# Conditioned transformer block and rotation: the first batch's projections and maxima are moved in the program order

## The reference, cut to what matters

```python
ada = silu(c) @ W_ada + b_ada
shift_msa, scale_msa, gate_msa, shift_mlp, scale_mlp, gate_mlp = split(ada, 6)
h = layernorm(x) * (1 + scale_msa) + shift_msa
x = x + gate_msa * attention(h)          # softmax(q k^T / 3) v, 16 heads, then W_proj
h = layernorm(x) * (1 + scale_mlp) + shift_mlp
x = x + gate_mlp * (gelu(h @ W_fc1 + b_fc1) @ W_fc2 + b_fc2)
U, _ = qr(P)                             # P: 144 x 64
R = expm(A(silu(cond) @ W.T + b))        # A: skew-symmetric 64 x 64 for each batch
x_rot = x + (x U R - x U) U^T
```

## Time and profile before

| what | value |
|---|---|
| median of 3 runs | 350.19 us (350.04 to 352.31) |
| the profiled execution: its time | 352.32 us |
| the profiled execution: its span, first to last instruction | 350.5 us |
| PE busy | 288.3 us (82%), 2717 matmuls |
| DVE busy | 244.1 us (70%), 762 instructions |
| ACT busy | 145.0 us (41%) |
| POOL busy | 120.3 us (34%) |
| mean granted TensorE clock | 0.974 |

### The profile page before, as it was taken

The page is one execution under the profiler, slowest core; times in us unless marked ns, Lnnn a source line. Parts: engine busy times, 40 slices in busy tenths (PEclk is TensorE's granted clock), DMA queues, the critical chain, the costliest instruction groups (busy, mean ns, idle before and its releaser), DMA issues.

```text
span 350.5 us, 7754 instructions
## 1 busy us (share of the span) xinstructions
PE 288.3 (82%) x2717; PEld 175.1 (50%) x2717; DVE 244.1 (70%) x762; ACT 145.0 (41%) x270; POOL 120.3 (34%) x307
## 2 busy tenths in 40 slices
PE   2897877598987877879888879888987999999774
PEld 1333443254434443545455545555756666666662
DVE  6758656866767888976888978986565555665541
ACT  2212102377776474544455554555431332122211
POOL 6730820700602639333525316233043433310010
PEclk9999999999899999987999999999999999999995
DMA  4924230231551232220221210000000000000013
GB/s 124 287 61 137 57 91 9 51 79 37 131 160 29 60 88 46 56 74 17 67 75 34 72 52 3 4 2 3 2 2 1 1 2 0 3 0 2 0 35 102
DMA packets 20285, 18.00 MB, mean 51 GB/s; under 512 B 3541, under 2 KB 18087, under 8 KB 20122
## 3 DMA queue, kind: packets, MB, share of 16 engines
q1 hardware_dynamic: 19314, 16.31, 17.2%
q10 hardware_dynamic: 934, 1.21, 1.2%
HBM read 12.32 MB, written 4.81 MB: 49 GB/s over the span
## 4 chain that ended last, share of the span: by engine, by line
PE 48%; DVE 40%; issue 6%; ACT 3%; POOL 1%; DMA 0%; DVEq 0%; ACTq 0%; POOLq 0%
DVE nm L958 15%; PE ps L463 6%; PE m L497 6%; DVE gp L765 5%; PE pst L277 4%; PE m L299 4%; PE m L672 4%; PE m L283 3%; DVE gm L766 3%; PE pst L394 3%; PE pst L484 3%; DVE qst L801 2%; DVE piv L800 2%; PE pst L278 2%; DVE pm L795 2%
## 5 line engine op out<-in xcount | busy, mean ns | idle before, releaser
L958 DVE TENSOR_REDUCE nm<-ps 128x2 f32<-128x512 f32 x128 | 87.6, 688 | 33.2 <-PE ps L463 29.2
L1196 ACT ACTIVATE pex<-pst 128x1024 f32<-128x1024 f32 x64 | 65.6, 1025 | 28.2 <-PE pst L484 24.3
L463 PE MATMUL ps<-ks,qs 54*128 54x256 bf16 x256 | 28.1, 297 | 27.0 <-DVE nm L958 26.3
L497 PE MATMUL m<-pex,ve 128*32 128x256 f32 x512 | 36.0, 401 | 0.0
L795 DVE TENSOR_SCALAR pm<-m 64x1 f32<-64x1 f32 x64 | 13.6, 212 | 29.0 <-PE m L299 28.4
L1518 POOL TENSOR_TENSOR xin<-xin,res 128x288 f32<-128x288 f32 x16 | 12.7, 793 | 59.0 <-DVE res L987 59.0
L463 PEld LDWEIGHTS ps<-ks,qs 54*128 54x128 bf16 x256 | 10.3, 98 | 41.5 <-issue 36.8
L283 PE MATMUL m<-gm,ident 64*64 64x65 f32 x126 | 24.0, 278 | 7.0 <-DVE gm L766 3.9
L484 PE MATMUL pst<-qs,ks 56*128 56x256 bf16 x256 | 26.3, 284 | 1.4 <-ACT pex L1196 1.2
L283 PEld LDWEIGHTS m<-gm,ident 64*64 64x64 f32 x126 | 14.1, 157 | 26.3 <-issue 19.1
L1496 POOL TENSOR_TENSOR qkr<-qk,parts 96x768 f32<-96x768 f32 x6 | 9.8, 1637 | 46.5 <-ACT parts L1177 34.0
(11 more groups left out here) (253 smaller groups left out, 572.7 us busy)
## 6 DMA issues: line engine op xcount, KB each, us to landing
scr_qk<-parts SPq DMA_DIRECT2D x24, 144.0 KB, 2.0
qs<-scr_qk SPq DMA_DIRECT2D x96, 36.0 KB
ks<-scr_qk SPq DMA_DIRECT2D x72, 36.0 KB
gates<-scr_ada SPq DMA_DIRECT2D x2, 576.0 KB, 6.1
out_dram<-xin SPq DMA_DIRECT2D x8, 144.0 KB, 2.0
wr<-in_L_cond_W_dram SPq DMA_DIRECT2D x1, 1134.0 KB
xin<-in_x_dram SPq DMA_DIRECT2D x1, 864.0 KB, 5.4
ks<-scr_qk ACTq DMA_DIRECT2D x24, 36.0 KB
```

What stands on the lines that cost most here:

```text
L463: ins = mm(ps[e][:, L * i:L * i + L], qs[64 * e:64 * e + KS, b % 3, 2 * g + i, 128 * lt:128 * lt + 128], ks[64 * e:64 * e + KS, b % 3, 2 * ...
L497: last = mm(m[32 * j:32 * j + 32, 0:L], ve[:, t % 3, mt, 4 * g + j, :], pex[:, n % 4, 2 * e + i, :], start=(mt == 0), stop=(mt == LT - 1))
L958: nc.vector.tensor_reduce(nm[:, lt, e, 2 * g:2 * g + 2], ps[e][:, :].rearrange("p (h l) -> p h l", h=2), AX.X, ALU.max, negate=True).then_ ...
L1196: nc.scalar.activation(pex[:, n % 4, :, :], pst[0][:, :, :], ACT.Exp, scale=ATT_SCALE).then_inc(s("exp_done"), 1)
```

## The change

The number of chain steps in the prologue falls from 14 to 9. All 8 slots of turn -1 get one (before: the last 4), and the MLP half starts with 4 instead of 3, so that step 85 comes at its first turn as before; in turns 0 to 7 each slot holds the step that the slot before it held. On PE and DVE the first batch's three q and k chunks follow one another with no chain step between them, and so do the remainders and the split; the second batch's projections come after, one chunk for each of steps 3, 4 and 5. Its remainders and its split move from ahead of turn -1 into that turn's slots 0, 1 and 2. `values(0)` is cut in halves over slots 0 and 1; `values(1)` moves to turn 0, slot 2; the second `wrT` moves from slot 1 to slot 0 of turn 0. `modulation_rests` and ACT's copy of `msr` move into slot 2 of turn -1. GpSimd's memsets of `ve` move from the start to behind `normalise(1)`.

```diff
@@ -44,3 +44,3 @@
 
-    PROLOGUE_STEPS = 14
+    PROLOGUE_STEPS = 9
     N_BASIS = 6
@@ -48,3 +48,3 @@
     TAIL_STEPS = 7
-    FIRST_STEPS = 3
+    FIRST_STEPS = 4
 
@@ -231,4 +231,4 @@
 
-            at = PROLOGUE_STEPS + (t + 1) * NS + n - NS // 2
-            return range(at, at + 1) if (t, n) >= (-1, NS // 2) and at < CHAIN else range(0)
+            at = PROLOGUE_STEPS + (t + 1) * NS + n
+            return range(at, at + 1)
 
@@ -236,6 +236,6 @@
 
-            at = PROLOGUE_STEPS + NS // 2 + B * NS + (FIRST_STEPS + TAIL_STEPS * t if t >= 0 else 0) + i
+            at = PROLOGUE_STEPS + (B + 1) * NS + (FIRST_STEPS + TAIL_STEPS * t if t >= 0 else 0) + i
             return range(at, at + 1) if at < CHAIN else range(0)
 
-        BASIS_TURN = (R + 1 - PROLOGUE_STEPS - NS // 2) // NS
+        BASIS_TURN = (R - PROLOGUE_STEPS) // NS - 1
         EXPM = 3
@@ -247,3 +247,3 @@
 
-        TURNED = [(0, 7), (1, 6), (2, 5), (3, 5), (4, 5), (6, 5), (7, 5), (7, 6)]
+        TURNED = [(0, 7), (0, 5), (2, 5), (3, 5), (4, 5), (6, 5), (7, 5), (7, 6)]
 
@@ -431,2 +431,4 @@
                         pe.wait_ge(s("hTf_ready"), b + 1)
+                    elif b == 2:
+                        pe.wait_ge(s("wqk_stacked"), 4)
                 m = shared[bank]
@@ -441,5 +443,5 @@
 
-            def values(b, bank):
-                m = claim(pe, bank, "values", b)
-                for lt in range(LT):
+            def values(b, bank, halves=range(LT)):
+                m = claim(pe, bank, "values", b) if 0 in halves else shared[bank]
+                for lt in halves:
                     rows = slice(128 * lt, 128 * lt + 128)
@@ -449,3 +451,4 @@
                     last = project(m[:, C * lt:C * lt + C], hTa[:, b % 2, rows], hTr[:, b % 2, rows], wqkv_a[:, 2 * C:3 * C], wqkv_r[:, 2 * C:3 * C])
-                filled(last, "values", b)
+                if LT - 1 in halves:
+                    filled(last, "values", b)
 
@@ -534,8 +537,10 @@
                     if t == -1:
-                        if n == 0:
-                            values(0, 6)
-                        if n == 1:
-                            values(1, 7)
+                        if n < LT:
+                            values(0, 6, (n,))
+                        if n == 2:
+                            modulation_rests()
                         if n == 4:
                             shift(0, 0, 5)
+                    if t == 0 and n == 2:
+                        values(1, 6)
                     if n == 0 and real(t - 1):
@@ -605,17 +610,11 @@
                     transpose_h(0, 6)
-                if k == 3:
                     pe.wait_ge(s("wqk_ready"), 8)
                     qk("qk2", (2,), 0, 7)
-                if k == 4:
-                    qk("qk01", (0,), 0, 5, 0)
-                if k == 6:
-                    qk("qk01", (1,), 0, 5, 1)
+                    qk("qk01", (0, 1), 0, 5)
                     transpose_h(1, 6)
-                if k == 7:
-                    modulation_rests()
-                if k == 8:
+                if k == 3:
                     qk("qk2", (2,), 1, 7)
-                if k == 10:
+                if k == 4:
                     qk("qk01", (0,), 1, 5, 0)
-                if k == 12:
+                if k == 5:
                     qk("qk01", (1,), 1, 5, 1)
@@ -623,3 +622,2 @@
             pe.wait_ge(s("identb_ready"), 1)
-            pe.wait_ge(s("wqk_stacked"), 4)
             pe.wait_ge(s("hTf_ready"), 2)
@@ -711,2 +709,3 @@
             transpose_h(B + 2, 5)
+            chain(mlp_steps(-1, 3))
             for t in range(B):
@@ -1010,2 +1009,9 @@
                         by_token(t - 1, 1)
+                    if t == -1:
+                        if n == 0:
+                            rest_of("qk2", 1, 2, 1)
+                        if n == 1:
+                            rest_of("qk01", 1, 0, 2)
+                        if n == 2:
+                            split(1)
                     if n == 3:
@@ -1046,9 +1052,5 @@
                     statistics(range(2, 4), "mv_ready")
-                if k == 3:
-                    batch_rows()
-                if k == 4:
-                    rest_of("qk2", 0, 2, 1)
                     dve.wait_ge(s("pT_filled"), 1)
                     nc.vector.tensor_copy(pT[:, :], ps[0][0:R, 0:C]).then_inc(s("pT_ready"), 1)
-                if k == 6:
+                    rest_of("qk2", 0, 2, 1)
                     rest_of("qk01", 0, 0, 2)
@@ -1056,10 +1058,8 @@
                     last_channels(1)
-                if 7 <= k < 11:
-                    if k == 7:
+                if k == 3:
+                    batch_rows()
+                if 4 <= k < 8:
+                    if k == 4:
                         dve.wait_ge(s("x1_loaded"), 16)
-                    statistics(range(4 + 3 * (k - 7), 7 + 3 * (k - 7)), "mv_ready")
-                if k == 10:
-                    rest_of("qk2", 1, 2, 1)
-            rest_of("qk01", 1, 0, 2)
-            split(1)
+                    statistics(range(4 + 3 * (k - 4), 7 + 3 * (k - 4)), "mv_ready")
             for t in range(-1, B):
@@ -1221,7 +1222,7 @@
                     if t == -1:
-                        if n == 0:
-                            evac_values(0)
                         if n == 1:
-                            evac_values(1)
+                            evac_values(0)
                         if n == 2:
+                            act.wait_ge(s("msr_filled"), 1)
+                            nc.scalar.copy(msr[:, :, :, :].rearrange("p b i c -> p (b i c)"), st_bank[0][:, :]).then_inc(s("msr_ready"), 1)
                             stack_of_k(1)
@@ -1229,2 +1230,4 @@
                             shift(0, 0)
+                    if t == 0 and n == 2:
+                        evac_values(1)
                     if n == 0 and real(t - 1):
@@ -1263,9 +1266,7 @@
             evac_hT(1)
-            act.wait_ge(s("msr_filled"), 1)
-            nc.scalar.copy(msr[:, :, :, :].rearrange("p b i c -> p (b i c)"), st_bank[0][:, :]).then_inc(s("msr_ready"), 1)
             stack_of_k(0)
             high_part("qk2", 1, 2, 1)
+            high_part("qk01", 1, 0, 2)
             act.wait_ge(s("wstack_loaded"), 7 * 16)
             by_dimension(wqk_r, wqkv_r, "wqk_stacked")
-            high_part("qk01", 1, 0, 2)
             for t in range(-1, B):
@@ -1541,5 +1542,2 @@
             nc.gpsimd.memset(hTf, 1.0).then_inc(s("hTf_one"), 1)
-            nc.gpsimd.memset(ve[:, :, :, :, :], 0.0).then_inc(s("ve_zeroed"), 1)
-            pool.wait_ge(s("ve_zeroed"), 1)
-            nc.gpsimd.memset(ve[:, :, :, :, D:D + 1], 1.0).then_inc(s("ve_zeroed"), 1)
             nc.gpsimd.memset(onesb[:, :], 1.0).then_inc(s("ones_ready"), 1)
@@ -1560,2 +1558,5 @@
             normalise(1)
+            nc.gpsimd.memset(ve[:, :, :, :, :], 0.0).then_inc(s("ve_zeroed"), 1)
+            pool.wait_ge(s("ve_zeroed"), 1)
+            nc.gpsimd.memset(ve[:, :, :, :, D:D + 1], 1.0).then_inc(s("ve_zeroed"), 1)
             pool.wait_ge(s("mv_ready"), 6)
```

6 lines of the change are left out of this document (3 added, 3 removed).

## The result

| | median of | executions | us |
|---|---|---|---|
| before, as shown above | 3 | 350.04 to 352.31 | 350.19 |
| before, beside the changed kernel | 4 | 350.04 to 352.31 | 351.16 |
| changed | 4 | 354.87 to 357.60 | 356.51 |

What follows compares the result with a forecast made beforehand. No engine is full, so time was taken as a sum of hand-overs between engines. The terms -1.85, -1.2, +0.95, +0.75 and +1.4 sum to +0.05, put on the median of 350.19: 350.2, range 346.3 to 353.5.

Steps and rivals of the forecast that it cites:

- Start, -1.85: Kernel start: without the `ve` memset DVE's first operation ends earlier, first projection from 15.06 to 13.2; bounds 0 to 2.05.
- Prologue and turn -1: -1.2 more: DVE's first maximum at 35.5, much of that gain lost in turn -1; bounds -3.1 to +0.6.
- both waits: Turn -1: PE starts slot 4's maxima 0.6 late behind GpSimd; ACT's `evac_hT(2)` waits for GpSimd's constants, charged 0.55.
- Turn 0, +0.95: Turn 0: `values(1)` in slot 2 costs +2.0, moving one `wrT` to slot 0 gives -1.05.
- The wait of 2.10: DVE's idle time ahead of turn 0 slot 2's maximum; moving a `wrT` into slot 0 was to take 1.05 off.
- my slower rival (0.12): Turn 0: the clock rises two slots later, each slot of 2.6 grows by 2; 354.2, chance 0.12.
- Basis, +0.75: Turns 5 and 6: basis norms one slot later make PE wait 1.4 in turn 6's slot 1, half hidden; bounds 0 to 1.4.
- MLP entry, +1.4: Ahead of the MLP's turns: the added chain step repeats a round over DVE with PE idle; bounds 0.9 to 1.6.
- Elsewhere the order is the same, so I let later work move as one block.: Stretches whose order is unchanged, say turns 1 to 4, keep their length; a change by over 1 would be wrong.
- The sum: Whole kernel: -1.85 - 1.2 + 0.95 + 0.75 + 1.4 = +0.05 on a span of 350.5.
- I put the difference on the median: Whole time: the +0.05 is added to the median of 350.19, not the profiled 352.32, giving 350.2.

Runs made afterwards that it cites:

- the fillers: Eight unused bf16 matmuls per slot in turn -1's PE waits: on the changed kernel 351.47 and 349.49; with values(1), steps and norms also moved, 346.87 and 344.69.

## Why the prediction was wrong

- **Start, -1.85.** Right as a mechanism, and in size for the memset alone (-1.70). In the first profile only -0.8 came, since `hb` met GpSimd's subtraction; over four profiles the first projection is 1.55 earlier on average. What I left out is that `hb` moved into other GpSimd work, and that DVE's first operation has more than one outcome even with the memset in place.
- **Prologue and turn -1.** DVE's first maximum at 35.5 was forecast; the four profiles give 35.8 on average. From the first projection to it the forecast had 22.3, and all four profiles have 22.3. Slot 4, both waits, and turn 0's start (3.05 earlier forecast, 3.0 measured) were right in the first profile. In two others slot 7 took 2.68 and not 5.09, since DVE came ahead of GpSimd, and turn 0 began almost 7 earlier.
- **Turn 0, +0.95. This step failed.** The wait of 2.10 fell to 1.26, -0.84 of the -1.05. But `values(1)`, taken at 2.0 between bounds of 1.1 and 3.1, made the slot 4.7 to 4.8 longer in three of four profiles and 1.6 in one. The bounds held only the work moved in. With the clock still low behind it, the rest of the slot was paid at 1.2 GHz too: L500 1.94 for 1.07, L351 1.10 for 0.65, the maxima 0.64 for 0.39, together 1.6. It is close to my slower rival (0.12), which put it down to a PE gap in slots 1 and 2. No gap was needed: PE was busy without a break from 65.1 to 76.3, the rise, all at the low clock.
- **Basis, +0.75.** PE waits for GpSimd 1.4, as forecast, in every profile. With the clock up, the stretch is nonetheless 0.4 shorter than before (14.56 for 14.94); with the low clock that followed the wait in three of four it is 1.1 longer. The mean of +0.8 fits the forecast by accident.
- **MLP entry, +1.4.** The round costs 1.4, as forecast. Missing were the 1.5 of low clock behind PE's gap, there in all four; the sum has no term for it.
- **"Elsewhere the order is the same, so I let later work move as one block."** This failed as well. The block's length varies by 2.9 between profiles of the changed kernel alone (by 3.5 with the kernel before), with the clock's falls in it, and the stretch to the end by 3.3. A forecast to 1 us can't be had from one profile here, and a range of 7 us was less than the spread of single executions alone (8 to 10).
- **The sum.** In the first profile, relative to my terms: start and prologue 0, turn 0 +3.0, turns 1 to 5 -1.5, basis +0.4, entry +1.5, end 0: +3.4 over a forecast of +0.05. The clock is behind 2.7 of the +3.0 and behind the +1.5. That the turns give back 1.5 goes with the falls in them; no edit is known to do it. The median missed by more, 356.5 for 350.2: 2.1 of that is the step "I put the difference on the median", since I took the median of three, 350.19, as the base beside the profiled 352.32, and 0.6 is the changed kernel's median above its profiled execution.

What stays open is what makes the clock rise where it does. With the fillers it rose early in 4 of 4 profiles, yet 13.6 us of unbroken work did not end a low clock. It also stays open why the first four executions all lay above 354.8, where 15 of 36 later ones did: another draw, or that chip.
